# Attention values in 64x64 array tiles, and x rounded by ScalarE

## What is computed

```python
q, k, v = [split_heads(jnp.einsum('bfe,ed->bfd', x, W)) for W in (W_query, W_key, W_value)]
scores = jnp.einsum('hbqd,hbkd->hbqk', q, k)
attn = jax.nn.softmax(scores, axis=-1)
out = jnp.einsum('hbqk,hbkd->hbqd', attn, v)          # heads are joined again
return jax.nn.relu(out + jnp.einsum('bfe,ed->bfd', x, W_res))
```

## Time and profile before

| | us |
|---|---|
| median of 3 runs | 1503.88 (1503.87 to 1504.69) |
| the profiled execution | 1503.88 |
| its span | 1502.1 |

### The profile page before, as it was taken

One profiled execution on the slowest core, in us unless ns is written; L12 is line 12 of the kernel. 1 busy time (PEld: TensorE's weight loads), 2 busy tenths in 40 slices (PEclk: granted clock), 3 DMA queues, 4 the chain that ended last, 5 costly groups with the idle time before them and its releaser, 6 DMA issues.

```text
span 1502.1 us, 73982 instructions
## 1 busy us (share of the span) xinstructions
PE 1483.0 (99%) x31232; PEld 1340.6 (89%) x31232; DVE 1390.9 (93%) x1793; ACT 1045.8 (70%) x1794; POOL 871.2 (58%) x1548
## 2 busy tenths in 40 slices
PE   7999999999999999999999999999999999999997
PEld 5999999999999999999999999999999999999996
DVE  6999999999999999999999999999999999999996
ACT  4677777777777777777777777777777777777775
POOL 3655555555555555555555555555555555555555
PEclk9999999999999999999999999999999999999999
DMA  3444444444444444444444444444444444444442
GB/s 58 99 85 97 86 97 86 97 86 96 86 97 86 97 86 96 86 96 86 97 86 96 86 96 86 96 87 96 87 96 86 96 87 96 87 95 87 95 87 76
DMA packets 677301, 135.35 MB, mean 90 GB/s; under 512 B 545888, under 2 KB 677216, under 8 KB 677216
## 3 DMA queue, kind: packets, MB, share of 16 engines
q1 hardware_dynamic: 675840, 134.30, 43.1%
q10 hardware_dynamic: 1376, 0.26, 0.1%
HBM read 67.37 MB, written 67.11 MB: 90 GB/s over the span
## 4 chain that ended last, share of the span: by engine, by line
PE 98%; issue 0%; POOL 0%; DVE 0%; ACTq 0%; ACT 0%; DMA 0%; POOLq 0%
PE ps_so L238 18%; PE ps_pt L229 17%; PE ps_so L217 14%; PE ps_vr L206 8%; PE ps_qk L193 8%; PE ps_qk L195 8%; PE ps_vr L208 8%; PE ps_qk L194 8%; PE ps_vr L207 8%; POOL y L154 0%; DMA w_raw<-in_L_rec_W_res_dram 0%; ACTq L327 0%; POOL v_diag L167 0%; ACT qk L284 0%; DVE row_max L357 0%
## 5 line engine op out<-in xcount | busy, mean ns | idle before, releaser
L154 POOL TENSOR_TENSOR y<-attn,vr 128x256 f32<-128x256 f32 x512 | 386.1, 775 | 523.8 <-DVE attn L372 500.2
L167 POOL COPY v_diag<-vr 64x264 f32<-64x264 f32 x1024 | 478.9, 468 | 102.9 <-POOL y L154 39.9
L304 ACT ACTIVATE probs_t<-ps_pt 128x512 f32<-128x512 f32 x512 | 307.4, 600 | 172.1 <-PE ps_pt L229 172.1
L357 DVE TENSOR_REDUCE row_max<-ps_so 128x16 f32<-128x1024 f32 x256 | 313.5, 1225 | 59.8 <-PE ps_so L217 59.5
L291 ACT COPY vr<-ps_vr 128x512 f32<-128x512 f32 x512 | 300.2, 586 | 62.0 <-PE ps_vr L208 1.4
L284 ACT COPY qk<-ps_qk 128x512 f32<-128x512 f32 x512 | 301.5, 589 | 48.8 <-PE ps_qk L195 9.2
L229 PE MATMUL ps_pt<-ident,shifted 128*128 128x128 f32 x2048 | 321.4, 279 | 0.8 <-ACT probs_t L304 0.8
L362 DVE TENSOR_TENSOR shifted<-ps_so,row_max 128x1024 f32<-128x1024 f32 x256 | 313.5, 1225 | 8.8
L238 PE MATMUL ps_so<-v_diag,probs_t 128*64 128x66 f32 x8192 | 296.1, 224 | 1.5 <-ACT probs_t L304 0.9
L238 PEld LDWEIGHTS ps_so<-v_diag,probs_t 128*64 128x64 f32 x8192 | 260.6, 137 | 36.4 <-issue 1.8
L206 PE MATMUL ps_vr<-w_hi,x_hi 128*128 128x256 f32 x1024 | 288.9, 282 | 0.0
(11 more groups left out here) (20 smaller groups left out, 1235.2 us busy)
## 6 DMA issues: line engine op xcount, KB each, us to landing
x_in<-in_r_x_dram SPq DMA_DIRECT2D x1024, 64.0 KB, 2.2
out_dram<-y SPq DMA_DIRECT2D x256, 256.0 KB, 2.5
w_raw<-in_L_rec_W_query_dram ACTq DMA_DIRECT2D x1, 64.0 KB, 2.2
w_raw<-in_L_rec_W_key_dram ACTq DMA_DIRECT2D x1, 64.0 KB, 2.6
w_raw<-in_L_rec_W_value_dram ACTq DMA_DIRECT2D x2, 32.0 KB, 2.6
w_raw<-in_L_rec_W_res_dram ACTq DMA_DIRECT2D x2, 32.0 KB, 2.5
```

What stands on the lines that cost most here:

```text
L154: nc.gpsimd.tensor_tensor(y[:, n % 2, a * HALF:(a + 1) * HALF].rearrange("k t (p j d) -> k j (t p) d", j=2, d=D), attn[:, n % 2, a * HALF: ...
L167: nc.gpsimd.tensor_copy(v_diag[n % 2][j * F:(j + 1) * F, seq, :, :, :, j].rearrange("k a t p d -> k a (t p) d"), vr[n][seq * F:(seq + 1) * ...
L357: nc.vector.reduce_max(row_max[:, :].rearrange("q (h u) -> q h u", h=HEADS), scores, AX_X).then_inc(max_ready, 1)
```

## The change

- The values: one matmul takes one head and one sequence, so 64 rows of keys, 64 queries as weights and 33 moving columns, in one of four 64x64 tiles of the array. Rows of head j and queries of sequence s give the tile. Their number per body goes from 16 to 32. Outputs of the two heads of a pair lie in different banks.
- The keys of head j, sequence s stand on partitions of half j in the transposed probabilities but on half s in `vr`. Where s is j, the matmul reads `vr` itself; where not, it reads `v_cross`, which GpSimd makes with two copies per body. `v_diag` and its clearing go. ScalarE's copy into `vr` waits also for `o_done` of the body that used the buffer.
- The waits in front of the values are in `wait_for_values` and stand before the last matmul of `project_vr`'s second half.
- `round_x` on ScalarE makes `x_hi(i + 2)` at the start of step i. VectorE keeps `rest_of_x(i + 2)` and then `transpose_x(i + 3)`, in this order.
- `attn` and `inv_sum` have the head of the pair ahead of the tile.

```diff
@@ gpsimd
                     for j in range(2):
-                        for m, seq in enumerate((1 - j, j)):
-                            nc.gpsimd.tensor_copy(
-                                v_diag[n % 2][j * F:(j + 1) * F, seq, :, :, :, j].rearrange("k a t p d -> k a (t p) d"),
-                                vr[n][seq * F:(seq + 1) * F, :, j].rearrange("k a t p d -> k a (t p) d"),
-                            ).then_inc(v_moved, 1)
-                            if m == 0 or j == 1:
-                                pool.wait_ge(v_moved, i * 4 + j * 2 + m + 1)
+                        nc.gpsimd.tensor_copy(
+                            v_cross[n % 2][j * F:(j + 1) * F].rearrange("k a t p d -> k a (t p) d"),
+                            vr[n][(1 - j) * F:(2 - j) * F, :, j].rearrange("k a t p d -> k a (t p) d"),
+                        ).then_inc(v_moved, 1)
+                        pool.wait_ge(v_moved, halves(i, j))
...
-            for n in range(2):
-                last = nc.gpsimd.memset(v_diag[n][:, :, :, :, :, :, :], 0.0)
@@ tensor
+            def wait_for_values(i):
+
+                if has(i - 1):
+                    pe.wait_ge(shifted_ready, i)
+                if has(i - 3):
+                    pe.wait_ge(attn_ready, i - 2)
+                if has(i - 2):
+                    pe.wait_ge(v_moved, halves(i - 2, 1))
+                    pe.wait_ge(pt_ready, halves(i - 2, 1))
...
                     nc.tensor.matmul(ps, x_hi[n][:, tok], w_vr_lo, start=False, stop=False)
+                    if (a, t) == (1, HALF - 1):
+                        wait_for_values(i + 1)
                     last = nc.tensor.matmul(ps, x_lo[n][:, tok], w_vr_hi, start=False, stop=True)
...
                             for s in range(SEQS):
-                                at = (a * HALF + t) * BANK + O_AT + p * 2 * VW
-                                last = nc.tensor.matmul(
-                                    ps_so[s * F:(s + 1) * F, at:at + 2 * VW],
-                                    probs_t[:, a, t * PAIRS + p, s * F:(s + 1) * F],
-                                    v_diag[n % 2][:, s, a, t, p].rearrange("k j d -> k (j d)"), start=True, stop=True)
+                                for j in range(2):
+                                    at = (j * 2 + a) * BANK + O_AT + (t * PAIRS + p) * VW
+                                    rows, queries = slice(j * F, (j + 1) * F), slice(s * F, (s + 1) * F)
+                                    if s == j:
+                                        values = vr[(n + 2) % RING][rows, a, j, t, p]
+                                    else:
+                                        values = v_cross[n % 2][rows, a, t, p]
+                                    last = nc.tensor.matmul(ps_so[queries, at:at + VW],
+                                                            probs_t[rows, a, t * PAIRS + p, queries], values,
+                                                            start=True, stop=True)
...
@@ scalar
                 if has(i - 4):
-                    act.wait_ge(v_moved, (i - 4) * 4 + 4)
+                    act.wait_ge(v_moved, halves(i - 4, 1))
+                    act.wait_ge(o_done, i - 3)
                     act.wait_ge(sum_ready, halves(i - 4, a))
...
+            def round_x(i, n):
+                act.wait_ge(xt_done, i + 1)
+                if has(i - 4):
+                    act.wait_ge(vr_done, halves(i - 4, 1))
+                nc.scalar.copy(x_hi[n][:, :], x_t[:, :]).then_inc(xhi_ready, 1)
...
             def step(i, n):
+                if has(i + 2):
+                    round_x(i + 2, (n + 2) % RING)
@@ vector
                 nc.vector.transpose(x_t[:, :], x_in[:, n % 2]).then_inc(xt_done, 1)
-                dve.wait_ge(xt_done, i + 1)
-                if has(i - 4):
-                    dve.wait_ge(vr_done, halves(i - 4, 1))
-                nc.vector.tensor_copy(x_hi[n][:, :], x_t[:, :]).then_inc(xhi_ready, 1)
+
+            def rest_of_x(i, n):
                 dve.wait_ge(xhi_ready, i + 1)
...
                 if has(i + 2):
-                    split_x(i + 2, (n + 2) % RING)
+                    rest_of_x(i + 2, (n + 2) % RING)
+                if has(i + 3):
+                    transpose_x(i + 3, (n + 3) % RING)
```

More of the change, by code:

```diff
@@ L66, in attention_program @@
         vr = [sb(f"vr{n}", [P, 2, 4, HALF, PAIRS, VW]) for n in range(RING)]
-        v_diag = [sb(f"v_diag{n}", [P, SEQS, 2, HALF, PAIRS, 2, VW]) for n in range(2)]
+        v_cross = [sb(f"v_cross{n}", [P, 2, HALF, PAIRS, VW]) for n in range(2)]
         row_max = sb("row_max", [P, HEADS * TILES])
@@ L71, in attention_program @@
         probs_t = sb("probs_t", [P, 2, HALF * PAIRS, P])
-        inv_sum = sb("inv_sum", [P, TILES, HEADS])
-        attn = sb("attn", [P, 2, TILES, HEADS, D])
+        inv_sum = sb("inv_sum", [P, HEADS, TILES])
+        attn = sb("attn", [P, 2, 2, TILES, PAIRS, D])
         ps_so = banks("ps_so", HEADS)
@@ L82, in attention_program @@
         ident_zero, ident_ready = sem("ident_zero"), sem("ident_ready")
-        ones_ready, diag_zero = sem("ones_ready"), sem("diag_zero")
+        ones_ready = sem("ones_ready")
         whi_ready, wlo_ready = sem("whi_ready"), sem("wlo_ready")
@@ L177, in _ @@
             last.then_inc(ones_ready, 1)
-            for n in range(2):
-                last = nc.gpsimd.memset(v_diag[n][:, :, :, :, :, :, :], 0.0)
-            last.then_inc(diag_zero, 1)
-            pool.wait_ge(diag_zero, 1)
             pool.wait_ge(ident_zero, 1)
@@ L236, in weigh_values @@
                             for s in range(SEQS):
-                                at = (a * HALF + t) * BANK + O_AT + p * 2 * VW
-                                last = nc.tensor.matmul(
-                                    ps_so[s * F:(s + 1) * F, at:at + 2 * VW],
-                                    probs_t[:, a, t * PAIRS + p, s * F:(s + 1) * F],
-                                    v_diag[n % 2][:, s, a, t, p].rearrange("k j d -> k (j d)"), start=True, stop=True)
+                                for j in range(2):
[8 more added lines that the diff above has]
+                                                            start=True, stop=True)
                 last.then_inc(o_done, 1)
             def step(i, n):
-                if has(i - 1):
-                    pe.wait_ge(shifted_ready, i)
-                elif not has(i):
-                    pe.wait_ge(shifted_ready, N)
-                if has(i - 3):
-                    pe.wait_ge(attn_ready, i - 2)
+                if not has(i - 1):
+                    wait_for_values(i)
                 if has(i - 2):
-                    pe.wait_ge(pt_ready, halves(i - 2, 1))
-                    pe.wait_ge(v_moved, (i - 2) * 4 + 4)
                     weigh_values(i - 2, n)
@@ L330, in _ @@
             nc.scalar.copy(w_hi[:, :, :], w_raw[:, :, :]).then_inc(whi_ready, 1)
+            for i in range(2):
+                round_x(i, i)
             act.wait_ge(ones_ready, 1)
@@ L337, in _, with transpose_x @@
         def _(dve):
-            def split_x(i, n):
+            def transpose_x(i, n):
                 dve.wait_ge(x_loaded[n % 2], dma_count(i, n, 4))
@@ L353, in step @@
                 scores = bank[:, :, 0:O_AT].rearrange("q h (u f) -> q h u f", f=F)
-                heads = bank[:, :, O_AT:O_AT + HEADS * VW].rearrange("q u (h d) -> q u h d", d=VW)
+                heads = bank[:, :, O_AT:O_AT + HEADS * VW].rearrange("q b (m d) -> q b m d", d=VW)
                 if has(i):
@@ L372, in step @@
                     nc.vector.tensor_tensor(
[L373 to L374 removed]
+                        attn[:, n % 2].rearrange("q j (a t) p d -> q (j a) (t p) d", a=2), heads[:, :, :, 0:D],
+                        inv_sum[:, :, :].unsqueeze(3).to_broadcast([P, HEADS, TILES, D]),
                         ALU.mult).then_inc(attn_ready, 1)
                 if has(i + 2):
[L377 removed]
+                    rest_of_x(i + 2, (n + 2) % RING)
+                if has(i + 3):
+                    transpose_x(i + 3, (n + 3) % RING)
             dve.wait_ge(whi_ready, 1)
@@ L381, in _ @@
                                     ALU.subtract).then_inc(wlo_ready, 1)
-            split_x(0, 0)
-            split_x(1, 1)
+            for i in range(2):
+                transpose_x(i, i)
+                rest_of_x(i, i)
+            transpose_x(2, 2)
             run(step)
```

4 lines of the change are left out of this document (1 added, 3 removed).

## The result

Time after: 1535.03 us median of 4 runs (1532.53 to 1536.19), against 1504.17 us (1503.87 to 1504.69) for the kernel before, measured again beside it. The ratio is 1.0203, 95% interval 1.0185 to 1.0220: the change makes the kernel 31 us slower. The profiled execution of after took 1535.18 us, 1533.4 of it in the span. The forecast was 1524, 20 us slower, with a range of 1494 to 1537.

What follows compares the result with a forecast made beforehand. TensorE was taken as the bound, with VectorE close behind; moved waits close a loop of 3.42 + .15 + .11 + .21 + 1.05 + .91 = 5.85 us against 5.77, +20 us over some 253 bodies: 1524 us, range 1494 to 1537.

Steps and rivals of the forecast that it cites:

- The values keep their pace: Value matmuls in four tiles: 16 passes a tile at .057 to .059 us as before, no gain.
- Rival 1: Values shorten to the scores' length, -.24 us a body, ScalarE's chain nearly the bound: 1463 us; chance .12.
- The switch out of the values: From last value matmul to first score: streaming 33 columns is shorter, gaining .03 us a body.
- The way of a common body: Attention product's end to last residual-value load: .10 us for the signal, matmul .06 late, in three bodies of four.
- The way of the body with the register operation: Product's end to last residual-value load in one body of four: .30 us, matmul .26 late.
- The sum: Steady body 5.85 us against 5.77, +.08 over some 253 bodies: +20 us, 1524 us.
- ScalarE not waited for: ScalarE's added cast of x, .62 us a body, is covered with .21 margin: cost 0, near 1200 us busy.
- VectorE's idle: VectorE's wait for the scores before the row maxima rises from .20 to about .7 us a body.
- Rival 3: All bodies take the long way (.30) from product to load, +.23 us a body: 1562 us; chance .06.
- Rivals 1, 2 and 4: Values shorten, 1463 us (.12); the wait costs nothing, 1496 (.16); tiles run two by two, 1740 (.02).
- Rival 4: The values' four tiles run two by two, .94 us more a body: 1740 us; chance .02.

Runs made afterwards that it cites:

- the two kernels above: Changed kernel with the four waits back before the values, work left out: 16 moving columns for 33, 1498.89 us; 32 weight columns for 64, 1410.96 us.
- The kernel with the loop cut elsewhere: Changed kernel with attn_ready as last of the four waits and TensorE's loop cut before the second half of the transposes: 1525.30 us, ratio 1.0142.
- the change alone: Kernel before with only the x part: ScalarE rounds x, VectorE transposes three bodies ahead; 1504.44 us, ratio 1.0001.
- the kernel with the waits alone: Kernel before with only the four waits moved in front of the last residual-value matmul: 1585.02 us, ratio 1.0535.
- A turn of 2464 TensorE instructions: Changed kernel with eight bodies in a turn of TensorE's hardware loop in place of four: 1999.32 us, ratio 1.3295.
- attn_ready last: Changed kernel with attn_ready written as the last of the four waits: 1531.20 us, ratio 1.0180.
- the waits back: Changed kernel with the four waits back before the first value matmul, an unused semaphore's increment between them and it: 1503.12 us, ratio .9987.

## Why the prediction was right, and where it was off

1. **The values keep their pace** (forecast: +-0): right in kind. They took .021 less a body (.937 to .916), not counted. Rival 1 asked for .24 less; the two kernels above show why it doesn't come. Most of the .021 lies in the first step from pass to pass of a tile: .108 before, .079 after and with 16 moving columns; every later step is some .058 in all three. What makes the first one long was not taken apart.
2. **The switch out of the values** (forecast -.03): wrong. It is .149 and .150, as if the shorter streaming of 33 columns didn't matter. With 16 columns it was .136, with 32 weight columns .122. I had split the .14 into streaming and switching by a difference of two rows; that split was an assumption.
3. **The way of a common body** (forecast .10 and .06 late): mis-sized. It is .07, nearer to the quicker of the two rows at the start of the program (.05 and .11), and the load's .11 didn't follow in full: in the median the matmul streams .08 behind the load and .15 behind the product, as before. The values begin .386 behind the product and not .360, so .026 late. With the .021 of point 1, a common body is 5.778 and not 5.773, close to nothing. The forecast had .06 for each of three bodies. TensorE's idle time was to be put down to the product; where it shows, in the other two bodies, the profile puts it down to "issue".
4. **The way of the body with the register operation** (forecast .30 and .26 late): right. .317, and the body is .25 longer. Over four bodies that is .063.
5. **The branch**: missing from the sum. The prediction placed one late body in four; there are two. Before, TensorE's sequencer ran ahead over the branch while the array worked off what was queued, then waited in front of the values (the branch ended .43 us ahead of the product). Now it waits one matmul earlier with the branch still to come, and one matmul of work can't cover it. Price .19, over four .047. The kernel with the loop cut elsewhere shows it by taking it away. The prediction did name what is queued behind the waiting load: the next body's matmuls, and not the branch.
6. **The sum**: forecast .065 (long) + .045 (common) - .03 (switch) = .08 a body. Measured .063 + .047 (branch) + .002 (common) = .112. Two terms that I counted weren't there, +.045 and -.03, and one that was there I didn't count. The 20 us of the forecast are so partly right by offsetting errors; with points 1 to 3 as measured it would have been .065, 16 us, and a reader should take the size as luck and the long way and the sign as the argument's. So it is with the range: 1535 lies 2 us inside its upper end, which was reached with longer ways and the lost gain of the switch, and not with a branch.
7. **The loop's entry**, +2.2 us once: not foreseen.
8. **ScalarE not waited for** (forecast near 1200 us busy): 1178.3, and the change alone measured 1.0001. Right. The margin was larger than I thought, since x_lo was shorter.
9. **VectorE's idle** before the row maxima (forecast .7): 1.12 a body. .20 + .46 (the cast) + .37 (shorter x_lo) + .11 (longer period) = 1.14.
10. Rival 3 (1562) is no case of this change, but it is what the kernel with the waits alone does (1585): the point from which it decides is whether something stands between attn_ready and the load, as it said. Rivals 1, 2 and 4 fell: the values aren't much shorter, the waits do cost, and the four tiles run together. (Rival 4's 1740 left out of its sum the .08 of the forecast; with it, it is 5.85 + .94 = 6.79, and 1762.)

## What to carry to other kernels

A wait that closes a loop between engines is cheapest directly in front of the first instruction that needs it, and with as much work as possible already queued for the array. Moved ahead by one matmul it lays open what the sequencer does behind it. Here the load came .32 behind the signal's source with a register operation in between, against .07 for the wait alone, and a loop's branch added .19. Small matmuls that follow each other in a tile went at the pace of their weight loads here (58 ns with 64 columns, 34 with 32), so count weight columns before you halve anything else; and put a loop's branch where the engine has work queued.

## What the runs showed of the hardware that I had not expected

- **Instruction supply can be the bound.** After with TensorE written out: +191 us over its looped form, with 140 us of "issue" before the scores; before written out: +5. A turn of 2464 TensorE instructions: 1999 us; of 1232: 1535.
- **The order of waits before one instruction** moved the load by .045 (.070 to .115) with the same four signals.
- **x_lo on VectorE** went from 1048 ns to 682, in after and with the rounding alone, for the same shape and types. It isn't the cast ahead of it that makes it long: with the same cast in front, the first four x_lo of the kernel before took 691 to 695 ns while GpSimd did nothing (one is in the earlier trace rows), and all later ones 1049 to 1059, with GpSimd's addition of y running for .9 us of them, begun .36 ahead. In after, x_lo begins .22 ahead of the addition and keeps its 682; the addition that starts under it takes 1007 ns in the median, where its like took 686 before. So of two operations that overlap, the later one was the longer. No run varied this overlap alone. The transpose stayed at about .70 and .71.
- **The edges of the hardware loop** cost 2.2 us in after, 1.9 with attn_ready last, 3.6 with the waits back and 8.3 with the loop cut elsewhere, and nothing in before, with the waits alone or with the rounding of x alone. The tiles bring 308 instead of 244 TensorE instructions a body; that the fetching of them is the cause is a guess.
- **Starts of the scores' passes**: 64 passes in eight tiles start within .697, so .011 apart.
- **The best kernel found**, the waits back with the rest kept, is 0.13% faster than before by the ratio above (1503.12 us), under the 0.2% that the prediction names as what can't be told from no change. Neither half of the change is worth its code here.
